# Full and pooled out products taken by turns in a windowed linear-attention kernel

## What is computed

```
qkv    = einsum('nchw,oc->nohw', xw, qkv_w)
pooled = avg_pool5(qkv)
q, k   = relu(q), relu(k);  v gets a 9th column of ones
kv     = einsum('ngld,nglm->ngdm', k, v)
out    = einsum('ngld,ngdm->nglm', q, kv)
out    = out[..., :-1] / (out[..., -1:] + 1e-15)
y      = einsum('nchw,oc->nohw', out, proj_w)
```

## Time and profile before

| | us |
|---|---|
| median of 3 runs | 805.83 (805.62 to 808.54) |
| the profiled execution's own time | 805.22 |
| its span, first to last instruction | 803.4 |
| TensorE busy | 766.7 (95%) |
| VectorE busy | 622.8 (78%) |
| GpSimd busy | 591.6 (74%) |
| ScalarE busy | 567.4 (71%) |

### The profile page before, as it was taken

How to read it: one execution, slowest core, us unless ns; L and a number is a source line. 1 busy time by engine, 2 the same in 40 slices (tenths; PEclk the granted TensorE clock), 3 DMA queues, 4 the chain that set the end, 5 groups by cost and what they waited for, 6 DMA issues and landing times. The chain is left out here.

```text
span 803.4 us, 62585 instructions
## 1 busy us (share of the span) xinstructions
PE 766.7 (95%) x28226; PEld 669.6 (83%) x28226; DVE 622.8 (78%) x1250; ACT 567.4 (71%) x1350; POOL 591.6 (74%) x1336
## 2 busy tenths in 40 slices
PE   0879999999999999999999999999999999999995
PEld 0668888888888888888888888888888888888884
DVE  7857888887768888888767888888777776767675
ACT  0557776768676777777676767677777767676773
POOL 0557877778787878787787878787877778787861
PEclk9999999999999999999999999999999999999998
DMA  7022131000012232000012222100000000000000
GB/s 298 3 63 59 59 89 40 30 29 21 29 59 82 66 89 59 30 20 30 23 47 70 77 75 74 49 20 29 20 30 20 30 26 24 30 20 30 20 30 31
DMA packets 20643, 38.74 MB, mean 48 GB/s; under 512 B 2416, under 2 KB 15216, under 8 KB 20592
## 3 DMA queue, kind: packets, MB, share of 16 engines
q1 hardware_dynamic: 20592, 38.25, 14.7%
HBM read 19.36 MB, written 18.87 MB: 48 GB/s over the span
## 5 line engine op out<-in xcount | busy, mean ns | idle before, releaser
L384 ACT ACTIVATE q_full<-ps,cst 128x384 f32<-128x384 f32 x192 | 103.7, 591 | 200.2 <-PE ps L706 200.2
L289 POOL TENSOR_TENSOR xd<-x_all,mean_t 128x384 f32<-128x384 f32 x95 | 78.8, 829 | 139.1 <-PE ps L716 119.3
L681 PE MATMUL ps<-wkv_sb,xn 128*128 128x256 f32 x576 | 142.9, 384 | 22.3 <-DVE xn L521 22.3
L267 POOL TENSOR_TENSOR x_all<-y_pool,x_all 128x96 f32<-128x96 f32 x380 | 148.2, 426 | 16.2 <-ACT y_pool L407 16.2
L681 PEld LDWEIGHTS ps<-wkv_sb,xn 128*128 128x128 f32 x576 | 102.9, 192 | 32.5 <-issue 22.3
L365 ACT ACTIVATE vm_pool<-ps,cst 128x256 f32<-128x256 f32 x288 | 119.5, 524 | 0.0
L571 DVE TENSOR_TENSOR x_all<-ps,x_all 128x384 f32<-128x384 f32 x96 | 53.5, 557 | 80.1 <-PE ps L797 80.0
L740 PEld LDWEIGHTS ps<-kvc_full,q_full 64*32 64x32 f32 x9216 | 88.1, 106 | 27.3 <-issue 27.3
L365 ACT ACTIVATE vm_full<-ps,cst 128x384 f32<-128x384 f32 x192 | 101.0, 579 | 4.6 <-PE ps L681 4.6
L740 PE MATMUL ps<-kvc_pool,q_pool 64*32 64x36 f32 x9216 | 100.3, 198 | 3.6 <-issue 3.6
L740 PE MATMUL ps<-kvc_full,q_full 64*32 64x36 f32 x9216 | 99.0, 198 | 1.5 <-ACT q_pool L384 1.5
(11 more groups left out here) (72 smaller groups left out, 1414.6 us busy)
## 6 DMA issues: line engine op xcount, KB each, us to landing
out<-x_all SPq DMA_DIRECT2D x96, 192.0 KB, 1.9
x_all<-x SPq DMA_DIRECT2D x36, 384.0 KB, 3.3
x_all<-x SPq DMA_DIRECT2D x6, 768.0 KB, 8.2
wkv_sb<-wkv SPq DMA_DIRECT2D x1, 128.0 KB, 10.8
wq_sb<-wq SPq DMA_DIRECT2D x1, 128.0 KB, 10.6
proj_sb<-proj SPq DMA_DIRECT2D x1, 128.0 KB, 10.5
cst<-consts SPq DMA_DIRECT2D x1, 90.0 KB, 10.9
bn_sb<-bn SPq DMA_DIRECT2D x1, 2.0 KB, 10.3
```

The lines of the kernel that those rows point to most:

```text
L267: return pool.tensor_tensor(o, a, b, ALU.add)
L289: link(pool.tensor_tensor(xd[:], x_all[:, s * SP:(s + 1) * SP], mean, ALU.subtract), 1)
L384: return act.activation(to, src, ACT.Relu, scale=col(mask))
L681: last = pe.matmul(ps[:, bank, at:at + 2 * P], xn[:, p, t * P:(t + 1) * P], wkv_sb[:], start=True, stop=True)
```

## The change

`out_products_of`, which did all products of one kind, becomes `out_pair`, which does those of one n. In every strip but the last, `out_products` calls it by turns: the four full products of n, then the four pooled products of n, for all 12 n. The full and the pooled kind each raise their semaphore with their own last matmul, so both now at n = 11.

The pooled products get `swap`: the column quad is 2g + 1 - j instead of 2g + j, so their places are (0, quad 1), (1, quad 0), (0, quad 3), (1, quad 2), those that the full products leave free. Their output thus stands with the two quads of a half swapped, and the pooled half of the projection's weights is swapped to match, on the host. The last strip keeps full and pooled apart (`out_products_last`). All waits stand for the same things as before, and all other stages keep their order on all engines.

```diff
-            def out_products_of(q, kvc, bank, pairs):
-
-                for n in range(HALF):
-                    half, e = divmod(n, pairs)
-                    for g in range(G):
-                        for j in range(QG):
-                            i, rows, z = g * QG + j, slice(H64 * j, H64 * (j + 1)), QS + n * QS + g * Q4
-                            last = pe.matmul(ps[Q4 * i:Q4 * (i + 1), bank, n * KC:(n + 1) * KC], q[rows, z:z + Q4],
-                                             kvc[rows, half % 2, (half // 2 * G + g) * pairs + e],
-                                             start=True, stop=True)
+            def out_pair(q, kvc, bank, pairs, n, swap):
+
+
+                half, e = divmod(n, pairs)
+                for g in range(G):
+                    for j in range(QG):
+                        i, rows, z = g * QG + (1 - j if swap else j), slice(H64 * j, H64 * (j + 1)), QS + n * QS + g * Q4
+                        last = pe.matmul(ps[Q4 * i:Q4 * (i + 1), bank, n * KC:(n + 1) * KC], q[rows, z:z + Q4],
+                                         kvc[rows, half % 2, (half // 2 * G + g) * pairs + e],
+                                         start=True, stop=True)
                 return last
...
             def out_products(s):
-                if is_first(s) or is_last(s):
+
+                if is_first(s):
                     out_wait(s)
                     pe.nop(nofuse=True)
-                out_products_of(q_full, kvc_full, OUTF_LAST if is_last(s) else OUTF, EF).then_inc(out_f, 1)
-
-            def out_products_pooled(s):
-
-                if is_last(s):
+                for n in range(HALF):
+                    full = out_pair(q_full, kvc_full, OUTF, EF, n, False)
+                    pooled = out_pair(q_pool, kvc_pool, OUTP, EP, n, True)
+                    if n == HALF - 1:
+                        full.then_inc(out_f, 1)
+                        pooled.then_inc(out_p, 1)
+
+            def out_products_last(s, pooled):
+
+                if pooled:
                     pe.wait_ge(kvc_p, s + 1)
-                    pe.nop(nofuse=True)
-                out_products_of(q_pool, kvc_pool, OUTP, EP).then_inc(out_p, 1)
+                else:
+                    out_wait(s)
+                pe.nop(nofuse=True)
+                for n in range(HALF):
+                    last = (out_pair(q_pool, kvc_pool, OUTP, EP, n, True) if pooled else
+                            out_pair(q_full, kvc_full, OUTF_LAST, EF, n, False))
+                last.then_inc(out_p if pooled else out_f, 1)
...
-    proj = np.asarray(L0_conv_proj_w).reshape(P, 2 * P)
+
+    proj = np.asarray(L0_conv_proj_w).reshape(P, 2, G, QG, Q4).copy()
+    proj[:, 1] = proj[:, 1, :, ::-1]
+    proj = np.ascontiguousarray(proj.reshape(P, 2 * P))
```

More of the change, by code:

```diff
@@ L819, in step @@
                 out_products(s)
-                out_products_pooled(s)
                 if is_first(s):
@@ L850, in _ @@
                 step(s + 1, 1)
-            out_products(NS - 1)
+            out_products_last(NS - 1, False)
             project_full(NS - 2)
-            out_products_pooled(NS - 1)
+            out_products_last(NS - 1, True)
             project_pooled(NS - 2)
```

## The result

| | us |
|---|---|
| changed kernel, median of 4 runs | 867.88 (866.04 to 871.13) |
| kernel before, beside it | 805.73 (805.54 to 808.54) |
| ratio, 95% interval | 1.077 [1.075, 1.080] |
| profiled execution of the changed kernel | 868.78, span 867.0 |

The change makes the kernel 62 us slower; 870 was predicted. Lines have moved by a few: the out products are L741 now, the kv products L729, the divide L595, L596 and L599.

The account below looks back on a forecast made before the run. TensorE, busy in every stage of a 7.91 us strip, was taken as the bound. Its uncovered wait for VectorE's full divide adds 0.68 us over 95 steps: 805.2 + 64.6 = 869.8, predicted 870 us, range 836 to 880.

Parts of the forecast that it names:

- pace of the even part: Out products after the first loads and a pause: still 24 loads in 0.20 us, 8.33 ns per load and matmul.
- out products, first to last start: Sign of being right: a strip's mixed out products take 1.6 to 1.7 us from first to last start.
- VectorE's idle time ahead of den_full: Sign of being right: VectorE's idle time before dividing the full products grows from 72 us to about 140.
- o_full ends, after the stage's first load: VectorE's multiply of the full products ends 0.73 us later, at 407.99 instead of 407.26.
- from o_full's end to the pooled kv matmul: TensorE's restart after a real stop, taken from the run's end: 0.15 us, so pooled kv products begin at 408.14.
- weights not loaded ahead: First pooled kv weights lead by 0.03 us after a stop instead of 0.07, leaving 0.04 us open per strip.
- The step that decided: Out products: last full pair is the 184th instead of the 96th, 88 pairs or 0.73 us later, delaying VectorE's divide.
- second stall: After the pooled kv wait, pooled q convolution and pooled projection find their inputs ready; no further stall was expected.
- taking no gain from the places: Out products on eight places: supply taken as the limit, so 192 pairs keep today's pace and nothing is gained.
- One of the signs named: Wait table lists TensorE's pooled kv products behind VectorE's o_full, about 95 times, 0.6 to 0.7 us each.
- one rival: First loads' 6.9 ns pace holds through the out products: 0.28 us gained, 0.40 lost per strip, 843 us; chance 10%.
- The loss from more streams in the array at once: Four more streams in the array during out products: costed at zero, upper end 0.05 us per strip.

Follow-up runs that it names:

- turns alone: Changed kernel without the swap: full and pooled by turns, pooled products on the same four places as the full ones; 866.89 us, ratio 1.075.
- the doubled columns: Out products with 72 moving columns instead of 36: kernel before 929.96 us, changed kernel 898.99 us.
- One turn: Changed kernel with turns for n = 0 only, then the other full, then the other pooled products; 806.41 us against 807.52, ratio 0.999.
- halving the columns: Kernel before with 18 moving columns instead of 36 in the out products; 809.12 us against 807.52, ratio 1.002.

## Why the prediction was right, point by point

| step | predicted | measured |
|---|---|---|
| pace of the even part | 24 loads in 0.20 us | 24 in 0.20 us |
| out products, first to last start | 1.6 to 1.7 us | 1.61 us, first to last load; 1.76 us to the next stage, 1.79 before |
| VectorE's idle time ahead of den_full | 72 to about 140 us | 144.9 us |
| o_full ends, after the stage's first load | 407.99 - 404.90 = 3.09 us | 404.33 - 401.24 = 3.09 us |
| from o_full's end to the pooled kv matmul | 0.15 us | 404.43 - 404.33 = 0.10 us |
| weights not loaded ahead | 0.04 us | pooled kv to q convolution 0.90 us, 0.85 before: 0.05 us |
| per strip | 0.68 us | 0.65 us |
| in all | 64.6 us | 62.2 us |

The step that decided, that by turns the full products end 88 pairs later and that nothing covers it, held to the hundredth of a microsecond. The sum is 2.4 us too high, mainly by the restart after the wait: 0.10 us, not the 0.15 us taken from the end of the run. No second stall came, as worked out. The reason for taking no gain from the places held too: with the places doubled (turns alone against the change) the pace stays. But one of its arguments was thin: that the four places can do more than they are given rested on 7.9 ns for the first 33 loads against 8.33 ns after them, a difference of 5%. Four places are thus nearly as slow as the even pace, and this difference alone could hardly tell which of the two sets it; that it came out so is in part luck. The Trainium skill, TensorEngine Tiling (Array Packing), Tiling Modes, which lists 64x32 as eight tiles that load and multiply in parallel, is borne out by the 33 loads in 0.14 us and by the doubled columns (31 us less by turns). It gave no time here, since the even part keeps 8.33 ns with four places and with eight.

One of the signs named was wrong: the table of waits does not list the pooled kv products behind VectorE's o_full but behind "issue". And one rival was priced off the mark: the pace of the first loads is not 6.9 ns at best but 4.2 ns with eight places; since it ends after 33 loads, the price did not matter. The loss from more streams in the array at once, put at nothing, did not show: turns on eight places and on four take the same time.

None of these versions beats the kernel before. One turn, 0.999 [0.997, 1.000], is no difference.

## What to carry to other kernels

Before mixing two groups of work so that an engine is filled better, look who waits for the end of the first group: mixed, it ends with the second, and what overlapped with the second stands open. Ask whether the resource that is doubled is the one that the stage waits for; the same order without the doubling (the turns alone) tells it in one run, while halving the columns would have left it open here. Use of free places of the array shortened the stage with 72 columns in each matmul and not with 36.

## What was not expected of the hardware

- The out-product stages of 36 columns looked at here begin with 33 pairs at a faster pace (4.2 ns with eight places, 7.9 with four; with 18 columns on four the 33 still take 0.25 us). Then they stop, however early these are done: the 35th load comes 0.28 us after the first with four places and with eight. Why was not tried.
- With 72 columns on eight places the loads stop for over 0.04 us after every 34.
- The q convolution put between the two kv stages, which makes three changes between 64x64 and 128x128 places out of one, costs 0.36 us per strip, 34 us in all, with no wait late. That the changes of size cost it is likely and not shown.
